# A two-layer transformer kernel: a straight-line attention stream with four score banks, expert indices copied one step early, and the second layer's last two phases made one

## The reference

```python
x = L0_attn_x                                   # (2, 2048, 512)
xn = _layernorm(x)
# layer 0, s: 16 heads of 32; a token sees the last 128 tokens and the first 16 of its sequence
mask = (ki <= qi) & ((qi - ki < WINDOW) | (ki < PERSIST))
attn = softmax(where(mask, q @ k.T * scale, -inf));   s = (attn @ v) @ Wo
# layer 0, g: 32 experts, each token goes to 6 of them, plus a shared expert
g = _silu(sum_k w_k * (silu(xn @ w_gate[e_k]) * (xn @ w_up[e_k])) @ w_down[e_k] + shared)
x = x + s * g
xn = _layernorm(x)
# layer 1, s: A is one row of 512 numbers for each batch (a sum of cosines of K and V over the tokens)
Y = A[:, None, :] * Q;   s = Y @ W_out + b_out + Xn      # Q = Xn @ Wq + bq
# layer 1, g: a gated network of 2048, and a routed one of 256 scaled by comb_w for each token
g = _silu((shared + routed * comb_w))
x = x + s * g
```

## Time and profile before

| | |
|---|---|
| three runs | 4780.84, 4772.49 and 4780.0 us, median 4780.0 us |
| profiled execution | 4768.42 us |
| its span | 4766.7 us |
| mean granted TensorE clock | 0.942 of 2.4 GHz |
| PE busy | 4248.5 us (89%) |
| PE weight loads busy | 3574.1 us (75%) |
| DVE busy | 2093.9 us (44%) |
| ACT busy | 1667.4 us (35%) |
| POOL busy | 1218.2 us (26%) |

### The profile page before, as it was taken

How to read it: one execution, slowest core, us unless ns; L and a number is a source line. 1 busy time by engine, 2 the same in 40 slices (tenths; PEclk the granted TensorE clock), 3 DMA queues, 4 the chain that set the end, 5 groups by cost and what they waited for, 6 DMA issues and landing times. The chain is left out here.

```text
span 4766.7 us, 72770 instructions
## 1 busy us (share of the span) xinstructions
PE 4248.5 (89%) x23087; PEld 3574.1 (75%) x23088; DVE 2093.9 (44%) x4013; ACT 1667.4 (35%) x3289; POOL 1218.2 (26%) x1802
## 2 busy tenths in 40 slices
PE   6964878869999999999995999998579999999998
PEld 5853666648888888888883777776368888888887
DVE  3455656644444444444442454453223334333333
ACT  2213656633333343343331333332123232222222
POOL 0002444424444444444441133333100000000000
PEclk8877999979999999999997999998789999999999
DMA  5775665645555555555543444332232323332321
GB/s 196 270 263 94 116 125 100 116 108 111 127 112 122 116 128 122 116 127 116 123 93 101 162 143 148 128 129 79 97 124 87 93 78 95 106 95 75 97 89 62
DMA packets 353789, 570.56 MB, mean 120 GB/s; under 512 B 33218, under 2 KB 199266, under 8 KB 348324
## 3 DMA queue, kind: packets, MB, share of 16 engines
q1 hardware_dynamic: 285124, 403.37, 29.5%
q0 software_dynamic: 68448, 164.35, 16.1%
HBM read 388.56 MB, written 179.06 MB: 119 GB/s over the span
## 5 line engine op out<-in xcount | busy, mean ns | idle before, releaser
L1485 POOL DMA_INDIRECT acc_d<-e_yw,e_to x208 | 331.7, 1595 | 361.8 <-ACT e_yw L1602 349.1
L1344 DVE TENSOR_TENSOR d_h<-d_sg,d_psU 128x512 f32<-128x512 f32 x144 | 99.0, 688 | 619.2 <-ACT d_sg L1302 619.2
L1211 POOL DMA_DIRECT2D out<-d_res x32 | 17.3, 542 | 1266.9 <-DVE d_res L1370 1205.2
L971 ACT ACTIVATE a_pr<-a_sm,a_nmax 128x272 f32<-128x272 f32 x512 | 263.8, 516 | 184.8 <-DVE a_nmax L1032 184.1
L1302 ACT ACTIVATE d_sg<-d_psG 128x512 f32<-128x512 f32 x144 | 86.1, 598 | 649.4 <-PE d_psU L108 649.3
L106 PE MATMUL e_psG<-e_gu,e_xT 128*128 128x352 f32 x832 | 286.7, 345 | 28.5 <-DVE e_xT L1650 28.3
L1032 DVE CUSTOM_DVE_ANT_0 a_sm<-a_psS,a_mask 128x272 f32<-128x272 f32 x512 | 213.1, 433 | 200.4 <-issue 175.1
L106 PE MATMUL d_psG<-d_x,d_gu 128*128 128x512 f32 x576 | 225.4, 391 | 65.4 <-DMA d_cmb<-comb_d 65.4
L1658 DVE TENSOR_TENSOR e_h<-e_sg,e_psU 128x352 f32<-128x352 f32 x208 | 108.4, 521 | 390.4 <-ACT e_sg L1615 390.4
L108 PE MATMUL e_psU<-e_gu,e_xT 128*128 128x352 f32 x832 | 268.6, 323 | 0.0
L106 PE MATMUL e_psU<-e_gu,e_xT 128*128 128x352 f32 x832 | 268.6, 323 | 0.0
(11 more groups left out here) (386 smaller groups left out, 11799.0 us busy)
## 6 DMA issues: line engine op xcount, KB each, us to landing
d_raw_gu<-in_wgu SPq DMA_DIRECT2D x146, 512.0 KB, 3.5
qk_d<-f_qk SPq DMA_DIRECT2D x32, 1024.0 KB
a_q<-qk_d SPq DMA_DIRECT2D x96, 256.0 KB, 5.4
a_k<-qk_d SPq DMA_DIRECT2D x96, 256.0 KB
e_rawgu<-in_w_gate SPq DMA_DIRECT2D x32, 704.0 KB, 6.0
e_rawgu<-in_w_up SPq DMA_DIRECT2D x32, 704.0 KB, 6.1
b_gu_raw<-in_wgu SPq DMA_DIRECT2D x40, 512.0 KB, 3.8
xT_d<-f_xT SPq DMA_DIRECT2D x16, 1024.0 KB
```

The lines of the kernel that those rows point to most:

```text
L971: act.activation(pr[half][:, h % HH, :], sm[s % SR][:, :], ACT.Exp, bias=nmax[s % SR][:, :], scale=-1.0, accum_out=rs[u % 2][:, h:h + 1]). ...
L1344: ins = dve.tensor_tensor(hv[m % 2][0:k, :], sg[m % 2][0:k, :], psU[m % 2][0:k, :], ALU.mult)
L1485: pool.indirect_dma_start(env.acc_d, bass.IndirectOffsetOnAxis(ap=to[:, :].bitcast(U32), axis=0), yw[:, :], None, compute_op=ALU.add).then ...
```

## The change

- **Route and attention.** `phase_attend` now calls `phase_route` and hands it three functions. SP issues the attention's first loads (queries and keys of three tiles, the persistent keys and values, masks, `Wo`) ahead of the zero fill; POOL, after its own few instructions of the route, clears the buffers and builds the persistent keys and values; ACT splits the upper part of `Wo` before its exponential of the route.
- **The attention's stream.** No loop: 32 tiles in a straight line, with constants in the waits. Four banks `psS` instead of three, one `psO` instead of two, values one step later, three query buffers. Turns are issued in pairs of heads (four transposes at once). The persistent probabilities and the inverse sums are turned over together at step 18, into a bank of `psP`, and the projection is cut into four pieces of three matmuls, at steps 26 to 29 instead of all at 25. The persistent keys of the second batch are copied while tiles 14 to 17 run.
- **Experts.** The copy of the next indices (`rows`) waits for the landing of the last gather and not for the transposes, and stands ahead of `weight`; `part()` stands directly behind ACT's copy of `xT`.
- **Last phase.** `phase_similarity`, the split of the down weights and `phase_ffn` for `d` become `phase_last`. The gate and up products start at once; the down weights are split block by block in the first group; the products for M stand in the stream of groups 0 and 4 (steps 12, 15, 18 and 21, the bias at 24), the four products with M at steps 30, 34, 38 and 42 of each group. There is one `psG` and one `psU` instead of two each, and M and the bias stay in SBUF.

```diff
-def phase_route(nc, env):
+def phase_route(nc, env, first_loads, first_built, first_split):
...
+            first_built(pool)
...
+            first_loads(sp)
             sp.wait_ge(c_ready, 9)
...
+            first_split(act)
             act.wait_ge(e_in, 1)
...
-    LAG = 4
-    SR = 3
+    LAG = 5
+    SR = 4
...
-        psO = [ps(f"a_psO{i}", [P, NGR, P]) for i in range(2)]
...
+        psO = ps("a_psO", [P, NGR, P])
...
-                    for offset, what in ((12, lambda u: pers_turn(u, 0)), (14, lambda u: pers_values(u, 0)),
-                                         (18, lambda u: pers_turn(u, 1)), (20, lambda u: pers_values(u, 1)),
-                                         (20, spread), (25, project)):
-                        if (u := tile_of(s, offset)) is not None:
-                            what(u)
-
-            with pe.Fori(0, B) as b:
-                body(b, b * BT)
...
+                if (u := tile_of(s, X_AT)) is not None:
+                    turn_sums(u)
+                if (u := tile_of(s, X_AT + 2)) is not None:
+                    pers_values(u)
+                    spread(u)
+                for c in range(KC):
+                    if (u := tile_of(s, X_AT + 8 + c)) is not None:
+                        project(u, c)
...
+            def rows(i):
+
+                if not isinstance(i, int) or i:
+                    pool.wait_ge(x_in, 16 * i)
+                    pool.sem_inc(passed, 1)
+                pool.tensor_copy(idx[:, :], env.ids[:, one(i)]).then_inc(idx_ready, 1)
+
             def gather(i):
+                pool.wait_ge(idx_ready, i + 1)
                 pool.wait_ge(xT_full, done(i - 1))
-                pool.sem_inc(passed, 1)
-                pool.tensor_copy(idx[:, :], env.ids[:, one(i)]).then_inc(idx_ready, 1)
-                pool.wait_ge(idx_ready, i + 1)
...
             with pool.Fori(1, end) as i:
                 gather(i + 3)
                 add(i)
+                rows(i + 4)
                 weight(i + 1)
...
                 act.activation(xT[0][:, :, :], psX[:, :, :], ACT.Copy).then_inc(xT_hi, 1)
+                part()
                 if old is not None or j:
                     hi_h(i - 1)
                 if old is not None:
                     weigh(i - 2)
-                part()
...
-        phase_similarity(nc, env)
-        phase_ffn(nc, env, "d", env.xT1_d, FB, P, env.wgu1, env.down1, env.out, True)
+        phase_last(nc, env)
```

More of the change, by code:

```diff
@@ L628, in _ @@
                 dve.tensor_copy(env.wslot[:, h * IDROW:(h + 1) * IDROW], pt[:, h, P:P + IDROW])
[L631 to L657, removed]
 def phase_attend(nc, env):
     ctx, sb, ps, sem = scope(nc)
-    U = BT
     R = 4
-    N = U * NH
+    QR = 3
+    N = TILES * NH
     HH = NH // 2
@@ L695, in phase_attend @@
[L695 to L701, removed]
+        rl = [sb(f"a_rl{i}", [P, P]) for i in range(2)]
         wo = [sb(f"a_wo{h}", [P, KC, D], F32R) for h in range(2)]
         wraw = sb("a_wraw", [P, KC, D])
-        y = [sb(f"a_y{i}", [P, D]) for i in range(2)]
@@ new lines, in phase_attend, with copied_out, bank, tile_of @@
+        order = {t: i for i, t in enumerate(turns)}
+        def copied_out(eng, u, p):
+            if p == HH:
+                eng.wait_ge(x_out, u + 1)
+            elif p in ON_DVE:
+                eng.wait_ge(pT_dve, u * len(ON_DVE) + ON_DVE.index(p) + 1)
+            else:
+                eng.wait_ge(pT_act, u * len(ON_ACT) + ON_ACT.index(p) + 1)
+        def bank(u, p):
+            return psP[order[u, p] % 2]
+        STEPS = range(N + 32 - NH)
+        def tile_of(s, offset):
+            u, rest = divmod(s - offset, NH)
+            return u if rest == 0 and 0 <= u < TILES else None
@@ new lines, in values @@
+            def values(u, g):
+                for p in (2 * g, 2 * g + 1):
+                    copied_out(pe, u, p)
+                if g == 0 and u:
+                    pe.wait_ge(o_ready, u)
+                for c, i in enumerate(slots(u)):
+                    for j in range(GH):
+                        h = GH * g + j
+                        ins = pe.matmul(psO[j * HD:(j + 1) * HD, g, :], vb[i][:, h, :],
+                                        pT[(u * HH + h // 2) % TR][:, (2 * (h % 2) + c) * P:(2 * (h % 2) + c + 1) * P],
+                                        start=(g == 0 and c == 0), stop=False, skip_group_check=True)
+                ins.then_inc(pv_done, 1)
@@ new lines, in _ @@
+            for s in range(SR):
+                score(s)
+            for s in STEPS:
+                if s + SR < N:
+                    score(s + SR)
+                if s < N:
+                    turn(s)
+                for g in range(NGR):
+                    if (u := tile_of(s, GH * g + GH - 1 + LAG)) is not None:
+                        values(u, g)
+                if (u := tile_of(s, X_AT)) is not None:
[6 more added lines that the diff above has]
+                        project(u, c)
```

1308 lines of the change are left out of this document (665 added, 643 removed).

## The result

The changed kernel takes 4633.64 us (median of four runs, 4628.72 to 4641.13), the kernel before 4777.69 us in the same runs: ratio 0.9701, 95% interval 0.9684 to 0.9718. That is 144 us, where 203 were forecast (4575); the range, 4520 to 4645, holds it. The profiled execution has a span of 4630.3 us, 136.4 less than that of before.

What follows compares the result with a forecast made beforehand. PE was taken as the bound: full in the last phase, waiting in attention and experts, idle between phases. Terms 22 + 25 + 66 + 20 + 68 = 201 us off 4768.4 gave 4567, written as 4575 for run medians; range 4520 to 4645.

Steps and rivals of the forecast that it cites:

- start of the attention: Attention's loads ahead of the zero fill: first score near 392 instead of 413.74, 22 us gained.
- the loop's second round: Attention loop between batches: straight-line code and spread key copies remove the emptied pipeline, 25 us gained.
- the tile, 31 times: Attention's steady tile: from 17.6 to 15.5 us as PE's waits on two late operands go, 66 us gained.
- experts: Experts' phase: gathers start about 1.0 us sooner after the earlier index copy, 20 us gained.
- last phase: Gated network d: earlier start, M's products added to the stream, shorter end; together 68 us gained.
- The sum for the range's lower end: Whole kernel: all terms near their good ends, 241 us, and 11 for the runs' offset, given as 4520.
- PE's own work and a tenth: Attention's tile: 15.5 us, taken as PE's busy 15.4 us plus a tenth once the waits go.
- at least 1.9: Attention, between spread and values: PE's scores and turns last at least 1.9 us, covering the 1.4 us until O is read.
- the prediction's own sign of being wrong: Attention: a new wait of PE on `a_o` above 0.5 us a tile would show the forecast wrong.
- a tile is bound by the ring: Attention rival: the PE, DVE, ACT, PE ring sets the tile, 17.0 us, gain 20 not 66, kernel 4621; chance 0.2.
- most such waits vanish: Experts: PE's gather waits, 0.75 us late on average, mostly vanish with gathers about 1.0 us sooner; 20 us.
- The step on the tail: End of last phase: four outputs leave 3.1 us apart; with four buffers some 4 us of this go.

Runs made afterwards that it cites:

- x3: Changed kernel with both experts' edits undone (index copy back in gather, ACT's part() back behind hi_h and weigh): 4647.0 us, ratio 0.9587.
- the control: The changed kernel as it is, run again on the later chip beside the follow-up kernels: 4649.08 us, attention 531.7 us.
- z1: Changed kernel with the persistent turn and inverse sums in psXY instead of a bank of psP: 4620.45 us, ratio 0.9516.
- y3: Changed kernel with two psO banks and three score banks, waiting for o_ready one tile later: 4694.87 us, ratio 0.9691.
- x1: Changed kernel with ACT's part() back behind hi_h and weigh, early index copy kept: 4646.47 us, ratio 0.9574.
- x2: Changed kernel with the index copy back in gather, waiting for the transposes, part() kept early: 4650.73 us, ratio 0.9582.
- x4: Changed kernel with PE's wait for exponentials in turn() moved behind the return, so even steps have none: 4655.92 us, ratio 0.959.
- y1: Changed kernel with the spread first and the persistent values one step later in the attention: 4643.32 us, ratio 0.9578.

## Why the prediction was right, and where its terms were off

The sign, the range and three of the five terms were right; the tile and the experts were not, and the sum was 59 us too large. On the first pair of traces:

| term | forecast | measured |
|---|---|---|
| start of the attention | 22 | 24.9 |
| the loop's second round | 25 | 25 |
| the tile, 31 times | 66 | 28 |
| experts | 20 | −5, and 0 by x3 against the control |
| last phase | 68 | 62 |
| between these, and `phase_mix` | 0 | +3.7, +3.0, +1.3, −6.8 |

The sum for the range's lower end is wrong in the prediction: 4768.4 − 241 + 11 is 4538 and not 4520. The measured time lies far above both. Of the last row, the 3.0 us lie between the last copy of y and the experts' first transposes, and the change made them: its last store leaves 1.0 us after that copy, and in both traces of before 3.9. No term of the prediction had them. The others lie in phases that nobody edited, and within what those phases varied by between traces of one code.

**Start.** Right in size, but by another end: the loads took 33 us, not 39, the fill landed at 382.2, and the route phase ended by DVE's chain and not by the fill. The chain itself took 62.3 us with POOL's build beside it (62.1 in the control), 62.0 without. The Trainium skill (SBUF — State Buffer, "SBUF: two separate sides") sets the lock between a GpSimd instruction that reads SBUF and a DVE instruction with two SBUF inputs, and this run hardly tests it: POOL's reading instructions ran from 327.23 to 336.57, and from 328.27 on DVE had `MAX8` and `FIND_INDEX8`, whose rows show one input. Only two of its two-input `TENSOR_TENSOR` stood beside a reading one of POOL, and they took no longer than before.

**The tile.** This is the step that was mis-sized, "PE's own work and a tenth". The two waits that the earlier trace rows named went or shrank, as said, and PE's own work even fell to 14.6 us a full tile, for 15.1 before in tiles at the upper level of the clock and 15.5 in all. But the idle time came back whole at two other places: ahead of the values, since O has been read 2.5 us after the spread's end (608.02 to 610.56) and not 1.4, and at the two psP banks, which the sums now share (z1 took that out). The 1.4 us of the earlier trace rows were read in the last tile, in which DVE has nothing else to do. The cover, "at least 1.9" us of PE's work between the spread and the values, measured 1.6 (608.02 to 609.64). So the prediction's own sign of being wrong, a new wait of PE on `a_o` above 0.5 us a tile, came true with 1.06 us, though the profile's row has another name for it. The rival "a tile is bound by the ring", given 0.2, came true in its size, at 16.7 instead of 17.0. Of the fourth bank the text said one sentence; y3 shows that a tile takes 1.55 us more where the bank goes to psO instead. That the measured time lies in the range is partly luck: on the first chip the tile gave less than half of its term.

**Where both runs of before differ** the tile's term is larger: 31 times 19.8 − 17.15 = 82 us on the later chips. The forecast of 66 stood between the two. It took the clock as given, 0.97, and put no term at what the clock gives back. On the first chip a full tile went from 17.78 to 16.91 us, and only 0.33 of these 0.87 us show between tiles at the upper level; on the later ones it is 1.97 of 2.81. The rest is the clock, which the changed stream holds at 1.00.

**Experts.** The step "most such waits vanish" failed. PE's waits for gathers went from 39 to 59, and from 29.3 to 40.4 us. Two errors: the gather's start isn't what sets its landing where PE waits (x1), and the new place of `part()`, costed at nothing by ACT's idle time, delays `weigh`, POOL's add and by it the gather (x2, one trace, 14 us against x3), while it saves some 2 to 9 us of PE's waits on `e_xT`. Together the two edits come to zero: 1483.3 us in x4 as in x3, of the same group.

**Last phase.** The start was right to the microsecond (11.7 for 11.5). From the first gate product to PE's last matmul the stream went from 1264.8 to 1304.1 us, and these are the two last ones:

```profile
4752.97 0.39 PE L108 MATMUL d_psU<-d_m,d_x 128*128 128x512 f32 x1
```

```profile
4617.45 0.39 PE L108 MATMUL d_psY<-d_wd,d_hT 128*128 128x512 f32 x1
```

It grew by 39.2 us, where M's products were counted at 36.6: 2.6 us too few, of which the first 387 us show 1.7 as idle. The step on the tail was wrong: from PE's last matmul to the end it was 13.8 us and is 12.9, 0.9 less and not 4. The outputs do leave 1.3 us apart for 3.1, but before, 24 matmuls with M stood behind the last down product, and the first output left at 4750.8, ahead of PE's end; now it leaves 2.8 us after the last matmul starts.

**What stays open.** Why the kernel before takes 19.8 us a tile on some chips and 17.6 on another: a DVE mask step starts 3.0 us after its score's record there (560.35 to 563.36), against 0.6 us on the first chip, and no row names what lies between. Matched one by one, the mask steps for which DVE had stood idle start at most 1.0 us after their score's record on the first chip, before and after. On the later chip 55 of 193 start over 1.5 us after it in the kernel before, up to 6.1, most of them for heads 12 and 13. In the control it is 32 of 184, one in nearly every tile, and this kernel's tile is 0.4 us longer there, all of it idle time of PE (2.7 for 2.3). The change is worth 144 us in one place and 205 in the other, and 56 of these 61 us lie in the attention (53 and 110). The POOL store that no longer waits for its landing, the split scatters and the constant waits weren't tried apart.

## What to carry to other kernels

A wait that is removed gives its time only if no other operand comes due within it: for each one list what ends next, in a steady iteration and not in the last one, in which engines are idle. Among buffers of one memory, give the spare one to the ring that all engines go round (here the scores, where the bank was worth 1.55 us of 17 more than in the other place, 0.5 of them without the clock), and let rare users share a bank that is idle at their step, not one in constant use. Compare two streams at the same level of the clock first, and then count in how many iterations it fell: an edit that shortens the iteration can lose it all there. An engine's idle time covers a moved instruction only if nothing queued behind it is on the path to a transfer.

## What the runs showed of the hardware

In the attention the clock fell in single tiles, to the lower of its two levels (1.2 for 2.4 GHz) and for a part of the tile. At the lower level the projection's matmuls started 0.43 us apart for 0.23, and a tile took 0.9 to 2.5 us more (means of the table above). The mean granted clock from 430 to 900 us was 0.88 to 0.95 before and 1.00 in the changed stream, but 0.98 in y1, whose tile was shorter and whose idle stretches were no longer than the control's, and 0.92 in y3. The same wait of 1.29 us stood in every tile of before on the first chip, and the clock fell in 6 of 28. Chips differ: one program with the same instructions took 4778 and 4853 us on two of them, nearly all of the difference in one phase (641.2 us for 571.8), while the changed one took 4634 and 4649. An unedited phase, `phase_mix`, varied by 15 us between profiled executions, which is more than several of the edits gave.
